# Order of output, key and score products on TensorE in the second block's cross attention

## The reference

```python
q = _split_heads(query @ Wq.T + bq)
k = _split_heads(key @ Wk.T + bk)
v = _split_heads(value @ Wv.T + bv)
scores = jnp.einsum('bhqd,bhkd->bhqk', q, k) * SCALE
scores = jnp.where(mask == 0, NEG_INF, scores)
attn = jax.nn.silu(scores)
out = jnp.einsum('bhqk,bhkd->bhqd', attn, v)
out = out.transpose(0, 2, 1, 3).reshape(B, Sq, HIDDEN)
return out @ Wo.T
```

## Time and profile before

| | |
|---|---|
| median of 3 runs | 2018.56 us (2017.13 to 2019.58) |
| profiled execution, its own time | 2012.08 us |
| its span, first to last instruction | 2010.4 us |
| mean granted TensorE clock | 0.987 |
| TensorE busy | 1888.9 us (94%) |
| VectorE busy | 1424.3 us (71%) |
| ScalarE busy | 1214.9 us (60%) |
| GpSimd busy | 561.5 us (28%) |

### The profile page before, as it was taken

How to read it: one execution, slowest core, us unless ns; L and a number is a source line. 1 busy time by engine, 2 the same in 40 slices (tenths; PEclk the granted TensorE clock), 3 DMA queues, 4 the chain that set the end, 5 groups by cost and what they waited for, 6 DMA issues and landing times.

```text
span 2010.4 us, 48604 instructions
## 1 busy us (share of the span) xinstructions
PE 1888.9 (94%) x17256; PEld 1509.8 (75%) x17256; DVE 1424.3 (71%) x3597; ACT 1214.9 (60%) x3994; POOL 561.5 (28%) x894
## 2 busy tenths in 40 slices
PE   7999999999999999999899999888887788899998
PEld 6888888888888888888677777666665555767775
DVE  6678878787878787677566756578787699544443
ACT  2676767676767677787545445277776566233333
POOL 2222222222222222121122211144544477111100
PEclk9999999999999999999999999899999899899999
DMA  7100000000000000000000000300000000000000
GB/s 229 30 2 2 1 2 1 2 2 2 2 2 2 2 2 2 2 2 2 1 1 1 1 1 1 102 10 2 2 2 8 22 17 2 1 0 11 11 6 16
DMA packets 30229, 25.73 MB, mean 13 GB/s; under 512 B 5276, under 2 KB 26788, under 8 KB 29992
## 3 DMA queue, kind: packets, MB, share of 16 engines
q1 hardware_dynamic: 29992, 22.62, 3.9%
HBM read 20.52 MB, written 2.10 MB: 11 GB/s over the span
## 4 chain that ended last, share of the span: by engine, by line
issue 50%; PE 20%; POOL 15%; POOLq 9%; PEld 3%; SPq 2%; DVE 1%; DMA 1%; DVEq 0%; PEldq 0%; ACT 0%
PE bank L1317 4%; PE bank L1309 3%; POOL X L2060 3%; POOL work L1119 3%; PE bank L2187 2%; PE bank L2174 2%; PE bank L2176 2%; SPq L2460 2%; PEld bank L1317 2%; POOL work L1851 2%; POOLq L1122 2%; POOLq L1096 1%; POOL H L1123 1%; POOL X L1861 1%; POOL work L1097 1%
## 5 line engine op out<-in xcount | busy, mean ns | idle before, releaser
L782 ACT ACTIVATE work<-bank,work 128x128 f32<-128x128 f32 x1024 | 367.0, 409 | 195.6 <-DVE work L880 195.6
L551 PE MATMUL bank<-work,wbig 128*128 128x128 f32 x2048 | 261.6, 276 | 2.5 <-ACT work L845 2.5
L782 ACT ACTIVATION_READ_ACCUMULATOR work<-bank,work 128x1 f32 x1024 | 252.7, 247 | 0.0
L551 PEld LDWEIGHTS bank<-work,wbig 128*128 128x128 f32 x2048 | 245.4, 193 | 3.0 <-ACT work L845 2.7
L887 DVE TENSOR_TENSOR work<-work 128x512 f32<-128x512 f32 x256 | 178.9, 699 | 20.1 <-issue 1.3
L797 ACT ACTIVATE work<-bank 128x512 f32<-128x512 f32 x256 | 173.6, 678 | 27.7 <-PE bank L564 27.7
L880 DVE TENSOR_REDUCE work<-bank 128x4 f32<-128x512 f32 x256 | 159.1, 686 | 33.5 <-PE bank L590 33.5
L564 PE MATMUL bank<-ident,work 128*128 128x128 f32 x1024 | 158.2, 277 | 17.9 <-DVE work L887 17.7
L564 PEld LDWEIGHTS bank<-ident,work 128*128 128x128 f32 x1024 | 113.9, 141 | 66.6 <-issue 40.5
L1383 ACT ACTIVATE work<-bank,col_b 128x512 f32<-128x512 f32 x128 | 87.7, 691 | 108.4 <-PE bank L1309 108.2
L2348 DVE TENSOR_TENSOR work<-wff,bank 128x320 f32<-128x320 f32 (+1 forms) x128 | 62.5, 489 | 124.3 <-ACT wff L2263 123.8
(11 more groups left out here) (343 smaller groups left out, 4101.6 us busy)
## 6 DMA issues: line engine op xcount, KB each, us to landing
wbig<-in_moe_w SPq DMA_DIRECT2D x2, 1536.0 KB, 9.4
work<-in_mask_l SPq DMA_DIRECT2D x8, 256.0 KB, 2.8
out<-X SPq DMA_DIRECT2D x8, 256.0 KB, 2.3
H<-in_moe_w SPq DMA_DIRECT2D x3, 512.0 KB, 8.6
wff<-in_moe_w SPq DMA_DIRECT2D x1, 1024.0 KB
X<-in_x SPq DMA_DIRECT2D x1, 512.0 KB, 4.2
wbig<-in_sa_wq SPq DMA_DIRECT2D x1, 512.0 KB, 3.7
wbig<-in_sa_wk SPq DMA_DIRECT2D x1, 512.0 KB, 4.5
```

Source lines behind the costliest of these rows:

```text
L551: last = nc.tensor.matmul(o[:, j * T:(j + 1) * T], w[:, t * 128:(t + 1) * 128], src, start=True, stop=True)
L782: last = nc.scalar.activation(at_probs[:, g, h, :], bank[g][:, h * T:(h + 1) * T], ACT.Exp, bias=at_nmax[:, g, h:h + 1], accum_out=at_den[ ...
```

## The change

In TensorE's loop of the cross attention `score` of sequence t + 1 is moved behind `output` of t - 1 and `key` of t + 2.

```diff
@@ attnx_pe
                     project(t + 2)
                 if t + 3 < B:
                     turn(t + 3)
-                if 0 <= t + 1 < B:
-                    score(t + 1)
                 if t >= 1:
                     output(t - 1)
                 if 0 <= t + 2 < B:
                     key(t + 2)
+                if 0 <= t + 1 < B:
+                    score(t + 1)
```

## The result

| | before | after |
|---|---|---|
| median | 2018.69 us (4 runs, 2017.13 to 2019.58) | 2003.32 us (4 runs, 2001.32 to 2005.46) |
| ratio, 95% interval | | 0.9923 (0.9909 to 0.9938) |
| profiled execution (its span) | 2012.08 us (2010.4) | 2003.11 us (2001.4) |

The change is faster by 15.4 us in the medians and by 9.0 us between the two profiled executions. (The median before is 2018.69 here, with a fourth run.)

A forecast was written before the change was run, and what follows sets the result against it. VectorE and TensorE waiting for each other, 4.44 us per step, were taken as the bound. Gains of 3.3 (first steps), 0.5 (next residual) and 5.7 (26 steps) sum to 9.5 us, from 2018.56 to 2009.1; range 2004 to 2014.5.

The forecast's parts named there:

- The first ring: VectorE's queries through project, turning, scores, output, residual and values: 4.44 us per step; without scores, VectorE's own work of 4.22.
- The 26 steps: Middle steps of the cross attention stage: 0.22 us gained per step, 5.7 in all, with 3.9 and 7.8 as ends.
- The step behind the first residual: First to second residual: 4.74 us before, 4.22 forecast after, a gain of 0.5.
- The second ring: ScalarE's silus, heads, then output, key, scores: 4.06 to 4.23 us per step; rival above 4.44 gives 2027, chance 0.05.
- The first steps: Stage's start to the first residual: earlier silus and weighing bring the first residual 3.3 us earlier.
- The step that failed: Total time: the 6.5 us between profiled execution and median kept, 9.5 off 2018.56 gives 2009.1.
- The clock rival: TensorE's clock stays up behind the gap before the second scores: first residual 0.6 us earlier, 2008.5, chance 0.08.
- Behind the stage: Filler passes ahead of the router's counts: in another execution up to 3.4 us less or more, low side widened to 2004.
- VectorE was not waiting: Rival: residual can't start sooner behind the masks, steps stay 4.44 us, only first steps gain: 2015.0, chance 0.12.

The follow-up runs named there:

- b_mask: Kernel before, with two of the four masks per sequence multiplying only half their columns: steps 4.440 us, one run of 2017.97 us.
- key_first: Kernel before with only the key product moved ahead of the scores: 2017.89 us in 12 runs, ratio 1.0002.
- a_mask: Changed kernel with two of the four masks per sequence multiplying only half their columns: steps 4.137 us, one run, span 2000.9 us.
- b_again: Kernel before, unedited, run and profiled again under a second label: 2017.46 us median in 12 runs, span 2015.6 us.
- a_head: Changed kernel with 23 TensorE filler passes at the stage's head and 8 ahead of the second scores: 2000.22 us in 6 runs, ratio to before 0.9941.
- a_again: Changed kernel, unedited, run and profiled again: 1999.99 us median in 5 runs, ratio to before 0.9919.
- out_first: Kernel before with only the output product moved ahead of the scores: 2018.09 us in 12 runs, ratio 1.0011.
- b_fill: Kernel before with 20 TensorE filler passes ahead of the second scores: 2014.13 us in 12 runs, ratio 1.0003.

## Why the prediction was right in its mechanism and wrong in its number

**The first ring: right.** Steps of 4.440 us became 4.188 (4.22 forecast). That the masks are outside it is shown by b_mask, that one product more lengthens it by just that product by key_first. The 26 steps gave 6.57 where 5.7 was forecast. Of the 0.9 that the term was short, 0.6 is this: VectorE has about 4.21 in three steps of four but 4.10 in the other, six times in the 26: the differences of the first residuals after are 4.21, 4.10, 4.22, 4.21. In the short step GpSimd first turns a mask (L2048), so that its scaling comes when the masks are nearly through, and they take 2.49 and not 2.58. Timeline of the changed kernel:

```profile
1601.48 2.01 POOL L2048 TENSOR_SCALAR work<-work 128x512 f32<-128x512 int32 x1
...
1603.32 2.49 DVE L2017 TENSOR_TENSOR work<-work 128x512 f32<-128x512 f32 x4
...
1605.20 1.28 POOL L2060 TENSOR_SCALAR X<-work 128x128 f32<-128x128 f32 x1 [0.18 <-issue]
```

The prediction had both lengths, and took the long one for every step. (The other 0.3 is 4.21 for 4.22 in each step.)

The step behind the first residual gained 0.22, not 0.5. It has 2.02 us from the residual to the next masks before and 2.01 after, where later steps have 1.72 and 1.70; the prediction took it for one of the later ones.

**The second ring: right, and near.** Forecast 4.06 to 4.23, measured 4.14 by a_mask. It was the term named as nearest to going wrong, and a change that moved the output product alone did fail by it (4.56).

**The first steps: the rival was right.** 3.3 us were forecast, with 0.6 more if the clock stayed up (chance 0.08). Behind the second scores it stayed up in every trace of the changed order (weighing 1.08), and where no passes filled it the gap before the second scores was 1.28 to 1.61, where 2.7 was forecast. The prediction counted the gap from the end of the first scores, and left out that the next turn's project, turning and key product run in between (1569.24 to 1570.50 in the trace after). The table load starts at 1568.41, right behind the keys and ahead of the scores' end, as forecast. The gain was 3.9 against the first trace, which is the 3.3 and the 0.6.

**The step that failed** is this one: "The median of the runs shown, 2018.56, lies 6.5 above the profiled one, and 9.5 off it". The 6.5 was carried over as a constant, and it is none: after the change it is 0.2. It was the distance between two groups of executions of the kernel before. b_again, of the upper group, is 5.2 us longer than the first trace: 3.2 of it to the first residual, where the 1.2 GHz stretch behind the gap of 3.15 us lasted through the third scores, 0.75 at the stage's end and 1.6 to the counts, less 0.3 ahead of the stage. The mean granted clocks say the same of the whole: 0.987 of 2010.4 us and 0.982 of 2015.6 us are some 20 us more at 1.2 GHz in b_again. The change shortens that gap, and with it goes the part in the first steps; the part behind the stage went too in these traces, for a reason that stays open (below). The first residual at 26.74 in b_again against 19.45 is 7.3 us of gain where the first trace had 3.9. The clock rival in the prediction priced the slow stretch from the one trace at hand, at 0.6; its price in b_again, of the upper group, is 3.2 more. The sign was there, in numbers that stood in the text (a profiled execution 5 us below the lowest of three runs), and it was taken as an offset.

**Behind the stage** the range left room for up to 3.4 us on the counts. The column is 25.86, 27.44, 29.12, 27.49, 27.45, 27.46 and, with 75 passes, 25.28 in the orders with the scores or one product ahead, and 25.86, 24.22, 22.59, 25.85 and, with 75, 23.67 and 23.66 in the changed one. So with 95 passes it is 27.5 on the mean in the one and 24.6 in the other. The granted clock there is 0.50 for a while in every trace, here b_again while it makes the router's products:

```profile
1728.00:1732.00 4.00, 4.00 (x22) 4.00 (x21) 0.69 (x1) 1.88 (x2) 0.00 (x0) 0.50 0.00 0
```

How long it is 0.50 between the transposes (L2140) and the counts gives the column, whatever the order. The first column here is read off the granted clock by short stretches; all executions have 95 passes:

| us at 1.2 GHz | to L2215 | executions |
|---|---|---|
| 3.4 | 22.59 | a_head |
| 6.8 | 24.22 | a_again |
| 10.2 | 25.85 to 25.86 | before, after, a_mask |
| 13.7 | 27.44 to 27.49 | b_again, key_first, out_first, b_mask |
| 17.1 | 29.12 | b_fill |

Each microsecond at 1.2 GHz costs 0.48 there; with 75 passes it is 23.66 and 23.67 at 10.2 and 25.28 at 13.7. So this part is the clock's alone. Why the order of an earlier stage should matter for how long the clock is down is not settled: before and after have the same 25.86. Traces this few can't tell a rule from chance, and no run here varied the start of that stage alone.

**The chances.** Faster had 0.87, and it was; "VectorE was not waiting" is refuted by the 4.19 and by b_mask. The range was too narrow at its low end, since all its terms were from one execution of a kernel whose executions differ.

## What to carry to other kernels

When an engine waits for an engine that waits for it, follow the ring once around in the timeline and add it up. The step is that sum, only a product inside it counts, and taking a product out is worth at most the distance to the next ring, here 0.25 of a product of 1.07. Moving two products that belong to two rings must be tried together, since each move by itself lengthened the step. And when the profiled execution is below every timed run, look for what differs between executions, the granted clock first, before using it as a constant: the same wait ahead of the same products was followed by slow stretches of different length.

## What was not expected of the hardware

The same gap of 3.15 us in the same code is followed by very different stretches of 1.2 GHz: one weighing and one project in the first trace of before, all work from the second to the third scores (1572.68 to 1581.7) in the second. The 29 runs beside it form two groups, 2009 to 2014 us at a mean granted clock of 0.987 to 0.988 and 2017 to 2020.5 us at 0.980 to 0.983, with nothing between; of 34 later runs three lie between them. The slow stretch accounts for 3.2 us of the distance; the rest is not traced.

TensorE was busy all the time and still granted 0.50: behind the stage it ran 24 passes of 8 columns (5.13 us) and transposes without a break, 4.00 of 4.00 us, at 1.2 GHz, in the kernel before as in the changed one. In the trace before, the clock fell at 1724.1, 7.6 us after TensorE had last been idle (0.86 us, ahead of 1716.46), and in b_fill it was 0.50 for 17.1 us of unbroken work. The Trainium skill, "TensorE: Matmul & The Clock Gate", Part 1, has idle time as what brings the half clock back; the gap of the first steps agrees with that, and these rows differ from it in that no idle time stands right before.
